# Layer 2 self-attention: scores issued last, and the softmax shares moved from GpSimd to VectorE

## The reference, cut to what matters

```
q, k, v = split(x @ w_qkv + b_qkv)          # 16 heads x 64
q, k    = q * cos + rotate_half(q) * sin, the same for k
p       = softmax(q k^T * scale + distance bias, causal)
out     = concat(p v) @ w_out + b_out
```

## Time and profile before

| what | us |
|---|---|
| median of 3 runs | 3091.52 |
| lowest and highest | 3089.79, 3096.44 |
| the profiled execution | 3087.09 |
| its span, first to last instruction | 3085.0 |
| the stage that is changed, within the span | about 1451 to 1960 |

### The profile page before, as it was taken

How to read it: one execution, slowest core, us unless ns; L and a number is a source line. 1 busy time by engine, 2 the same in 40 slices (tenths; PEclk the granted TensorE clock), 3 DMA queues, 4 the chain that set the end, 5 groups by cost and what they waited for, 6 DMA issues and landing times. The chain is left out here.

```text
span 3085.0 us, 40803 instructions
## 1 busy us (share of the span) xinstructions
PE 2376.2 (77%) x12384; PEld 1405.9 (46%) x12384; DVE 1795.4 (58%) x4355; ACT 1270.8 (41%) x2637; POOL 631.3 (20%) x583
## 2 busy tenths in 40 slices
PE   6864886668598888797788888676888789578487
PEld 4653651236423332564444444463444355557454
DVE  4665349979566555445444444346666634635777
ACT  3442346534354444222666666434444422123212
POOL 0410005534200000001555555431000000044100
PEclk7885987969699999798999999887999889688799
DMA  0000000010100000001222221100000000100000
GB/s 32 32 6 0 1 5 0 1 45 1 56 1 0 0 0 0 1 0 58 70 69 69 69 69 52 43 1 25 1 0 0 0 0 0 62 19 1 1 0 14
DMA packets 19881, 61.86 MB, mean 20 GB/s; under 512 B 4928, under 2 KB 4928, under 8 KB 18592
## 3 DMA queue, kind: packets, MB, share of 16 engines
q1 hardware_dynamic: 19488, 59.53, 6.1%
q10 hardware_dynamic: 256, 0.68, 0.1%
HBM read 42.37 MB, written 1.05 MB: 14 GB/s over the span
## 5 line engine op out<-in xcount | busy, mean ns | idle before, releaser
L824 ACT ACTIVATE PT<-P 128x512 f32<-128x512 f32 (+3 forms) x512 | 244.0, 516 | 231.9 <-PE P L496 122.1
L689 DVE TENSOR_REDUCE MF<-P 128x1 f32<-128x512 f32 (+3 forms) x512 | 281.7, 586 | 97.5 <-PE P L479 53.0
L2450 PE MATMUL P<-XT,W 128*128 x424 | 221.0, 617 | 63.4 <-ACTq L2484 63.4
L2526 DVE SCALAR_TENSOR_TENSOR X<-P,WE,X 128x128 f32 x576 | 162.2, 344 | 166.2 <-PE P L2467 161.6
L2467 PEld LDWEIGHTS P<-W,e_h 128*128 128x128 f32 (+1 forms) x1952 | 220.3, 190 | 61.0 <-issue 56.8
L2467 PE MATMUL P<-W,e_h 128*128 128x128 f32 (+1 forms) x1952 | 227.5, 277 | 3.4 <-DVE X L2526 3.4
L1286 POOL TENSOR_TENSOR d_e<-d_e,d_rc 128x512 f32<-128x512 f32 (+3 forms) x256 | 178.2, 723 | 219.2 <-DVE d_rc L1193 219.1
L2495 ACT ACTIVATE e_g<-P 128x512 f32<-128x512 f32 x148 | 88.4, 597 | 311.9 <-PE P L2450 311.9
L479 PE MATMUL P<-KA,QA 128*128 128x512 bf16 (+3 forms) x512 | 184.2, 366 | 25.5 <-ACT KA L808 15.1
L496 PE MATMUL P<-QA,KA 128*128 128x512 bf16 (+3 forms) x512 | 178.1, 354 | 32.3 <-ACT PT L824 12.7
L541 PE MATMUL P<-PT,VA 128*32 128x512 f32 (+3 forms) x1024 | 195.8, 518 | 0.0
(11 more groups left out here) (357 smaller groups left out, 4705.4 us busy)
## 6 DMA issues: line engine op xcount, KB each, us to landing
d_bt<-in_alibi SPq DMA_DIRECT2D x32, 512.0 KB, 3.6
d_moved<-d_raw SPq DMA_DIRECT2D x256, 64.0 KB, 2.0
W<-in_w_L_xattn SPq DMA_DIRECT2D x1, 4291.0 KB, 12.8
W<-in_w_L_ffn SPq DMA_DIRECT2D x1, 3333.0 KB, 11.3
W<-in_w_L_ffn SPq DMA_DIRECT2D x1, 3155.0 KB, 10.3
W<-in_w_L_attn SPq DMA_DIRECT2D x1, 2636.0 KB, 12.5
W<-in_w_L_ffn SPq DMA_DIRECT2D x1, 2310.0 KB, 8.9
W<-in_w_L_ffn SPq DMA_DIRECT2D x1, 1744.0 KB, 7.3
```

Of the source, the lines that this page charges most:

```text
L689: last = v.tensor_reduce(col, src, AX.X, ALU.max, negate=True)
L824: a.activation(k.PT[0:self.kp, h % self.slots, t, N - w:N], src, ACT.Exp, scale=self.scale).then_inc(s("exp_done"), 1)
L2450: pe.matmul(P[:, PG + j % 2, :], w["w1"][:, col:col + 128], x, start=True, stop=True).then_inc(s("gate"), 1)
L2526: last = v.scalar_tensor_tensor(x, y, k.WE[:, bass.ds(c * 4 + t, 1), e], x, ALU.mult, ALU.add)
```

## The change

On TensorE, the scores of step j are issued behind the transposes, values, result and weighted products of the same j, where they stood behind the transposes alone. On VectorE, each reciprocal is followed by a wait for itself and by two `tensor_scalar` instructions that make the shares in place; the reciprocal and these shares of step j-1 are now issued ahead of `biased` of step j. On ScalarE, the copy of the values is issued ahead of the exponentials of step 1. GpSimd keeps only the rotary additions.

```diff
@@ block.tensor @@
-                    if 0 <= n - 2 < ITEMS:
-                        scores(n - 2, j)
                     if j == 1 and 0 <= n - 2 < ITEMS:
                         values(n - 2)
                     if j == 1 and 0 <= n - 5 < ITEMS:
                         result(n - 5)
                     if 0 <= n - 4 < ITEMS:
                         weighted(n - 4, j)
+                    if 0 <= n - 2 < ITEMS:
+                        scores(n - 2, j)
@@ block.vector @@
                 v.wait_ge(s("exp"), 2 * (QT * n + j + 1))
-                if n >= 2:
-                    v.wait_ge(s("shares"), QT * (n - 2) + j + 1)
                 v.reciprocal(RC[:, n % 2, u, :], SM[:, n % 2, u, :]).then_inc(s("recip"), 1)
+                v.wait_ge(s("recip"), QT * n + j + 1)
+                for h in range(2):
+                    e = piece(n, h, u)
+                    last = v.tensor_scalar(e, e, RC[:, n % 2, u, h:h + 1], None, ALU.mult)
+                last.then_inc(s("shares"), 1)
...
-                    if 0 <= n - 2 < ITEMS:
-                        biased(n - 2, j)
                     if j >= 1 and 0 <= n - 2 < ITEMS:
                         recip(n - 2, j - 1)
                     if j == 0 and 0 <= n - 3 < ITEMS:
                         recip(n - 3, QT - 1)
+                    if 0 <= n - 2 < ITEMS:
+                        biased(n - 2, j)
@@ block.scalar @@
+                    if j == 1 and 0 <= n - 2 < ITEMS:
+                        values(n - 2)
                     if 0 <= n - 2 < ITEMS:
                         exponentials(n - 2, j)
-                    if j == 1 and 0 <= n - 2 < ITEMS:
-                        values(n - 2)
@@ block.gpsimd @@
-            def shares(n, j):
-                u = QT - 1 - j
-                g.wait_ge(s("recip"), QT * n + j + 1)
-                for h in range(2):
-                    e = piece(n, h, u)
-                    last = g.tensor_tensor(e, e, RC[:, n % 2, u, h:h + 1].to_broadcast([128, 128 * (u + 1)]), ALU.mult)
-                last.then_inc(s("shares"), 1)
-
...
-                    if j >= 1 and 0 <= n - 2 < ITEMS:
-                        shares(n - 2, j - 1)
-                    if j == 0 and 0 <= n - 3 < ITEMS:
-                        shares(n - 3, QT - 1)
```

## The result

| | median us | runs |
|---|---|---|
| before | 3093.39 | 4 (3089.79 to 3096.44) |
| changed | 3143.27 | 4 (3141.28 to 3147.63) |

The ratio is 1.0164, 95% interval 1.0146 to 1.0181. The change costs 49.9 us, where I had forecast 29.5 and a range that ended at 3142. The profiled execution has a span of 3139.2 against 3085.0. Some 8 us of these 54 lie ahead of the changed stage: GpSimd's first instruction in it starts at 1458.43 there and 1450.34 before, in stages that are the same in both.

A forecast was written before the change was run, and what follows sets the result against it. A cross-engine ring of 15.05 us a period was taken as the bound. Going to 16.25 over 27 periods gave +32.4, with ends +34.1, less 4.6 for slow stretches +29.5: 3121.0 us median, range 3102 to 3142.

The forecast's parts named there:

- The old ring opens: The 15.05 us cycle through TensorE, VectorE, ScalarE and GpSimd loses GpSimd's 2.75 us of shares; the rotary addition gains an iteration.
- The shares on VectorE: On VectorE, a pair of share instructions takes 0.40, 0.52, 0.66 and 0.78 us for 128, 256, 384 and 512 columns.
- The hold by GpSimd: VectorE's shares stand still while GpSimd's rotary addition executes, twice a period (j = 0 and j = 2), 1.09 us each.
- The chain alone: The dependent work on VectorE and ScalarE in one period, without waiting for GpSimd's additions: 14.07 us.
- The new ring: Period from biased step 2 through VectorE and ScalarE: 14.07 us of its own plus 2 x 1.09 blocked by GpSimd, 16.25.
- the sum: Added time: 27 full periods at 16.25 less 15.05 give +32.4 us; with other terms the total is +29.5.
- The short slow stretches: TensorE's spells at 1.2 GHz cost 9.2 us before; its longer idle time could hide some, so half, -4.6 us.
- the margin to the second scores: On TensorE, the second scores are ready at about 10.35 us, 0.15 ahead of VectorE's biased step 1.
- the ends: Items outside the 27 full periods: second and third +2.7 us, the 31st -1.9, last copies +0.9.
- more slow clock: Rival: a 1.2 GHz stretch on TensorE in every period adds up to 27 x 1.4 = 38 us, 3159; chance 0.05.
- No hold: Rival: GpSimd's additions do not delay VectorE's shares, TensorE sets 15.05 us a period, time 3089 us; chance 0.07.
- the faster side: Rival: shares undelayed and TensorE's path to second scores shorter, so 14.07 us sets the pace, about 3063 us; chance 0.04.

The follow-up runs named there:

- the repair: The changed kernel, with GpSimd's rotary additions also waiting until the shares of the same step are made: 3092.08 us, ratio 0.9991 to the kernel before.

## Why the prediction was wrong

- **The old ring opens.** Right. It sets 15.05 in the kernel before; with the shares alone moved it is gone, at 13.23. I wrote that the addition then has an iteration of slack. That is too much: it is needed by the next first scores, which in that run start 2.2 behind its end (1694.05 and 1696.26). That was enough.
- **The shares on VectorE.** Right. The groups by form give 484 ns at 512 columns, 351 at 256, and without the holds 417 at 384 and 284 at 128, for 480, 350, 420 and 290.
- **The hold by GpSimd.** Right in mechanism and place, and near in size: the held pairs take 1.51 and 1.77 where they take 0.48 and 0.75 without the addition, so 1.02 to 1.03 each, for 1.09. Taking it away brings 51 us (3143.27 to 3092.08), some of it by fewer falls. Measured with no clock falls on either side it is 16.10 less 14.79, 1.31 a period. The chain alone would have given about 2.05; the rest is TensorE, which sets 14.79 where I had 15.05. (My terms for that, 10.35 + 3.80 + 0.20 + 0.66, give 15.01. Measured are 10.14 and 4.65.)
- **The new ring.** 16.10 measured with the clock held up, 16.25 forecast. Over 27 periods that is 28.4 us, where the sum had 32.4.
- **The step that failed** is the term "The short slow stretches cost 9.2 before ... which can hide such a stretch. I take half, -4.6". The wait before the last scores doesn't hide the falls, it brings them. It was 2.58 long as I had worked it out, and behind it the clock fell in 21 of 27 periods, just where TensorE has little time to lose: the margin to the second scores was 0.15 by the forecast and about 0.3 in the run with the wait filled (10.42 less the 10.14 that TensorE needs). Mean 17.06 against 16.10 without falls is 0.96 a period, 26 us, in place of the 9.2 before: +17 where I had -4.6. That is 21 us more than forecast; the ring gives 4 back. The cost was 20 us above the forecast (49.9 and 29.5), so some 3 stay with the ends and the other stages, unresolved. The rival "more slow clock" was this mechanism, and I gave it 0.05, on the ground that the idle piece isn't much longer than the 1.75 of before. Its price of 1.4 a period was too high, its chance too low. What makes the falls so many stays open. The length of the wait alone doesn't: behind the 1.75 of the kernel before the clock fell in 6 of 27 periods, behind 1.72 in the kernel with the wait partly filled in 25 of 27.
- **No hold, and the faster side**: both wrong, the holds are in each period. Their period without holds, 15.05 by TensorE, was near the 14.79 that the repair shows. With the holds gone the time was 3092.08, near the 3089 of the rival, but partly by luck: that kernel still has falls in 13 of 27 periods.

## What to carry to other kernels

An instruction that is short on its engine can be the dearest in the kernel by its place: ask what stands behind it in its queue, and who waits for that. Try the parts of a change one by one before judging them; here each of two parts gained about 2%, and together they lost 1.6%. And a wait of TensorE, also one off the ring, can cost more than its length when its clock falls behind it. Here work of no use put into the wait paid, but only when it filled nearly all of it.

## What the runs showed of the hardware

- Repeated transposes that change no result made the kernel 21 us faster, since TensorE's clock stayed at 2.4 GHz. In the same kernel a wait of 2.58 us had a fall in 21 of 27 periods, one of 1.72 in 25, and one of 0.41 in none. With the additions late, 1.56 had one in 13 of 27. In the kernel before, 1.75 had one in 6 of 27, and in other orders the longest wait of 0.69 to 0.87 had one in none, one or two. So a wait of 1.7 us can bring a fall in nearly every period or in few. What of this is the length of the wait and what the work around it, these runs don't separate.
- GpSimd's additions get in ahead of VectorE's share by 0.03 us, in every full period, and the VectorE instruction ends 0.1 to 0.2 behind the addition's end. Of the addition's 1.26 us it loses 1.02. The custom instruction that reads PSUM and one SBUF tile ran in 0.41 beside the same additions, as fast as alone.
